# Metaformer block with a delta-rule mixer: the order of the first tiles' projections, statistics and norms around chunk 0

## The chip, the cores and the metric

One Trainium2 chip, one of its cores. Five engines run their own in-order instruction streams and meet at semaphores: TensorE (PE), VectorE (DVE), ScalarE (ACT), GpSimd (POOL) and the queue of DMA issues (SP). The metric is the device time of one execution in microseconds, and the figure given for a kernel is the median of its timed runs.

## The reference, cut to what matters

The input x is [8, 192, 16, 16]: 8 batches, 192 channels, 256 positions. All is float32.

```python
# 1. mixer: LayerNorm over channels, then a delta rule in 12 heads of width 16
q = l2norm(heads(silu(t @ Wq))); k = l2norm(heads(silu(t @ Wk)))
v = heads(silu(t @ Wv));         beta = sigmoid(t @ Wb)
# per head, for each position: u = beta*(v - S^T k);  S = S + k u^T;  o = S^T q
x = x + (t + o @ Wo)
# 2. feed-forward: LayerNorm, 8 experts with the top 2 taken, one shared expert of width 768
g = silu(x @ w_gate[e]) * (x @ w_up[e]);  routed = sum_e gate[e] * (g @ w_down[e])
out = x + alpha * shared + (1 - alpha) * routed
```

## The kernel before, in words

The 256 positions are cut into 16 **tiles** of 16 positions; a tile holds 8 batches x 16 positions, 128 tokens on the 128 partitions. All engines walk the same loop `chunks(step)` (L171), with c from -3 to 18. In step c, `at(d, fn)` works on tile c + d: the first norm and the projections run three tiles ahead of the recurrence (d = 3), the head norms two ahead (d = 2), the recurrence itself is chunk c (d = 0), and the feed-forward lags one to three chunks. The order of the work in a step is written out by hand for each engine, and since each engine is in order, an instruction that waits holds all that stands behind it.

**Front of a tile a.** ACT copies x (`A_xs`), PE transposes it (`A_x`, L363, L364; it waits until the v bank has been read, so for `A_z` and `A_silu_v` of the tile before), DVE takes statistics (`A_stats` L1125, `A_mean` L1129, `A_var` L1135), POOL makes the root (`rsqrt` L952), DVE the bias (`A_bias` L1142), ACT h and the residual (`A_plus` L594, `A_h` L585, `A_xh` L600), PE transposes h (`A_h` L355), ACT and DVE split it into a high and a low part (`A_hT` L608, `A_low` L1175), and PE projects: `A_vb` (v and beta, 5 matmuls of 204 columns) into one bank, `A_qk` (q and k, 5 matmuls of 384 columns) into another.

**Norms.** ACT: `A_silu_v` (L625, waits for DVE's `A_z` L1200, since both read the v bank), `A_silu_qk` (L617, L618), `A_sq` (L629); DVE sums the squares (`A_ss` L1206); ACT loads another table and makes the inverse norms (`A_inv`, L635 to L645); POOL scales: `A_kn` (ksc L928, kn L930), `A_vn` (L920), `A_klo` (L938, the low part of k), `A_qn` (L912). SP writes k to a scratch in HBM (L242) and reads it back in the layout of the recurrence as KR (L251), the same for q (L261, L273). The head of the queue is `load` (L286): tile 0's k and q with the feed-forward weights between and behind them; from c = 0 on each step issues tile c + 1's k, x or weights, and q.

**Recurrence.** PE spreads k over the partitions with `fill(c, f)` (L403), one for each pair of positions, f from 0 to 7, into two banks in turn; fill f waits until pair f - 2 is done. DVE then runs 16 positions of four operations: product (L1425), sum (L1427), product (L1429), state (L1433). They are numbered as slots 0 to 63, position i having slots 4i to 4i + 3, and `others(slot)` (L1310) puts DVE's work for other tiles behind given slots. In chunk 0, and in some slots later, each operation runs in two halves. Slot 8f needs fill f, so slot 40 needs fill 5. POOL multiplies states by q when half a chunk is done (`reading`, L963), and sums (`summing`, L970, L987) into oT, which DVE transposes in slot 23 of the next chunk (`Fa_otok` L1238); Wo, the second norm and the experts follow from it.

**Weights.** The experts' weights are split in high and low parts in the same opening: DVE's `split_up` (L1191 cast, L1193 subtraction), ACT's `weights_hi0` and `weights_hi1`, POOL's `weights_lo0` (L993) and `weights_1` (L998). They are placed by hand between the steps above.

The orders that the change touches are PE's for c < 0 (L472), ACT's for c = -2 (L758), POOL's for c = -1 and c = 0 (L1022, L1035), DVE's slots for c < 0 and c = 0 (L1316, L1335).

Of the kernel before, what the change touches and what calls it, by code (L numbers as in the profile page):

```python
# [34 lines left out]
def build(nc, x, Wq, Wk, Wv, Wb, Wo, router_w, w_gate, w_up, w_down, ws_gate, ws_up, ws_down, sg_w, sg_b, out):  # L35
    ctx = ExitStack()
    with ctx:
# [302 lines left out]
        def _(pe):  # L340
# [129 lines left out]
            def step(c, par):  # L470
                at = partial(stage, c, par)
                if c < 0:  # L472
                    at(3, A_x)
                    at(1, fill, 0)
                    at(1, fill, 1)
                    at(1, fill, 2)
                    at(3, A_h)
                    at(1, fill, 3)
                    at(3, A_vb)
                    at(1, fill, 4)  # L480
                    at(3, A_qk)
                elif c == 0:
                    at(3, A_x)
                    at(0, fill, 5)
                    at(0, fill, 6)
                    at(0, fill, 7)
                    at(1, fill, 0)
                    at(1, fill, 1)
                    at(3, A_h)
                    at(1, fill, 2)  # L490
                    at(3, A_vb)
                    at(3, A_qk)
                elif c < NC:
                    at(-2, Fb_up, 5)
                    at(0, fill, 3)
                    at(-2, Fb_up, 6)
                    at(-3, Fb_down, 4)
                    at(-1, Fa_o)
                    at(0, fill, 4)
                    at(3, A_x)  # L500
                    at(-2, Fb_turn, 0)
                    at(-1, Fa_y)
                    at(-2, Fb_up, 7)
                    at(-2, Fb_up, 8)
                    at(0, fill, 5)
                    at(-2, Fb_up, 9)
                    at(-2, Fb_up, 10)
                    at(-1, Fa_h)
                    at(-3, Fc_out)
                    at(-2, Fb_turn, 1)  # L510
                    at(-2, Fb_up, 11)
                    at(0, fill, 6)
                    at(-1, Fb_up, 0)
                    at(-2, Fb_turn, 2)
                    at(-2, Fb_down, 0)
                    at(0, fill, 7)
                    at(-2, Fb_down, 1)
                    at(-2, Fb_turn, 3)
                    at(-2, Fb_down, 2)
                    at(1, fill, 0)  # L520
                    at(-1, Fb_up, 1)
                    at(-1, Fb_up, 2)
                    at(3, A_h)
                    at(1, fill, 1)
                    at(-2, Fb_turn, 4)
                    at(-2, Fb_down, 3)
                    at(-1, Fb_up, 3)
                    at(1, fill, 2)
                    at(-1, Fb_up, 4)
                    at(3, A_qk)  # L530
                    at(3, A_vb)
                else:
                    at(-3, Fb_down, 4)
                    at(-2, Fb_up, 5)
                    at(-1, Fa_o)
                    at(-2, Fb_up, 6)
                    at(-2, Fb_turn, 0)
                    at(-1, Fa_y)
                    at(-2, Fb_up, 7)
                    at(-2, Fb_up, 8)  # L540
                    at(-2, Fb_turn, 1)
                    at(-3, Fc_out)
                    at(-2, Fb_up, 9)
                    at(-2, Fb_up, 10)
                    at(-1, Fa_h)
                    at(-2, Fb_down, 0)
                    at(-2, Fb_up, 11)
                    at(-1, Fb_up, 0)
                    at(-2, Fb_turn, 2)
                    at(-2, Fb_down, 1)  # L550
                    at(-1, Fb_up, 1)
                    at(-2, Fb_turn, 3)
                    at(-2, Fb_down, 2)
                    at(-1, Fb_up, 2)
                    at(-2, Fb_turn, 4)
                    at(-2, Fb_down, 3)
                    at(-1, Fb_up, 3)
                    at(-1, Fb_up, 4)
# [5 lines left out]
        def _(act):  # L564
# [179 lines left out]
            def step(c, par):  # L744
# [12 lines left out]
                    at(3, A_hT)  # L757
                elif c == -2:  # L758
                    at(3, A_xs)
                    at(2, A_silu_v)  # L760
                    at(2, A_silu_qk)
                    at(2, A_sq)
                    table(0, LN_EXP)
                    at(2, A_inv)
                    at(2, A_khi)
# [132 lines left out]
        def _(pool):  # L898
# [111 lines left out]
            def step(c, par):  # L1010
# [9 lines left out]
                    weights_lo0(5)  # L1020
                    weights_lo0(6)
                elif c == -1:  # L1022
                    rsqrt(c)
                    weights_lo0(7)
                    weights_lo0(8)
                    at(2, A_vn)
                    at(2, A_kn)
                    weights_lo0(9)
                    at(2, A_klo)
                    at(2, A_qn)  # L1030
                    weights_lo0(10)
                    weights_lo0(11)
                    weights_1(0)
                    weights_1(1)
                elif c == 0:  # L1035
                    weights_1(2)
                    weights_1(3)
                    at(0, reading, 0)
                    rsqrt(c)
                    weights_1(4)  # L1040
                    at(0, summing, 0)
                    at(2, A_vn)
                    at(2, A_kn)
                    weights_1(5)
                    at(2, A_klo)
                    at(0, reading, 1)
                    at(2, A_qn)
                    at(0, summing, 1)
                    weights_1(6)
                    weights_1(7)  # L1050
                    weights_1(8)
                elif c < NC:
                    once(c, 1, weights_1, 9)
                    at(-2, hidden, 6)
                    if c <= NC:
                        rsqrt(c)
                    at(-2, hidden, 7)
                    once(c, 1, weights_1, 10)
                    once(c, 1, weights_1, 11)
                    at(0, reading, 0)  # L1060
                    at(-2, hidden, 8)
                    at(-2, hidden, 9)
                    at(-2, hidden, 10)
                    at(0, summing, 0)
                    at(2, A_kn)
                    at(-2, hidden, 11)
                    at(2, A_qn)
                    at(-1, hidden, 0)
                    at(0, reading, 1)
                    at(0, summing, 1)  # L1070
                    at(2, A_vn)
                    at(-1, hidden, 1)
                    at(-1, hidden, 2)
                    at(-1, hidden, 3)
                    at(-1, hidden, 4)
                    at(-1, hidden, 5)
                    at(2, A_klo)
                else:
                    at(-2, hidden, 6)
                    if c <= NC:  # L1080
                        rsqrt(c)
                    at(-2, hidden, 7)
                    at(-2, hidden, 8)
                    at(-2, hidden, 9)
                    at(-2, hidden, 10)
                    at(-2, hidden, 11)
                    at(-1, hidden, 0)
                    at(-1, hidden, 1)
                    at(-1, hidden, 2)
                    at(-1, hidden, 3)  # L1090
                    at(-1, hidden, 4)
                    at(-1, hidden, 5)
# [20 lines left out]
        def _(dve):  # L1113
# [193 lines left out]
            def step(c, par):  # L1307
                w.clear()

                def others(done):  # L1310

                    def at(slot, d, fn, *args):
                        if done == slot:
                            stage(c, par, d, fn, *args)

                    if c < 0:  # L1316
# [3 lines left out]
                        at(11, 2, A_low)  # L1320
                        if c == -1 and done == 12:
                            split_up(3)
                        at(17, 2, A_z)
                        if c == -1 and done == 18:
                            split_up(4)
                        at(24, 3, A_stats)
                        at(27, 3, A_mean)
                        at(28, 3, A_var)
                        if c < -1:
                            at(35, 2, A_ss)  # L1330
                            at(48, 3, A_bias)
                        if c == -2 and done == 50:
                            split_up(0)
                            split_up(1)
                    elif c == 0:  # L1335
                        at(1, 1, A_ss)
                        at(3, 2, A_bias)
                        at(10, 1, A_vT)
                        at(20, 2, A_low)
                        at(27, 2, A_z)  # L1340
                        at(36, 3, A_stats)
                        at(38, 3, A_mean)
                        at(39, 3, A_var)
                        at(43, 2, A_ss)
                        at(50, 3, A_bias)
                    elif c < NC:
                        at(8, 2, A_low)
                        at(19, 2, A_z)
# [125 lines left out]
```

## Time and profile before

| | us |
|---|---|
| median of 3 timed runs | 482.03 (480.83 to 482.60) |
| the profiled execution | 479.88 |
| its span in the trace | 478.1 |
| first product of chunk 0 on DVE | 28.41 |
| DVE busy, of the span | 420.2 (88%) |
| POOL busy | 407.4 (85%) |
| PE busy | 414.6 (87%) |
| ACT busy | 345.8 (72%) |

The page's row of DVE by tenths in 40 slices of 12 us is `4489989999999999999999999999999999996200`. It is filled from the third slice on, and empties in the last three. The opening, from 0 to about 78 us, is where the change lies. To read it, take the timeline of one engine, name each instruction's tile by its place in the order written out above, and look at the bracket behind it: the idle time before it and what ended that.

### The profile page before, as it was taken

To read this page: it belongs to the slowest core of one execution; us is meant where nothing else is said; L and a number is where in the kernel's file an instruction comes from. 1 tells how busy PE (TensorE), PEld (TensorE's weight loads), DVE (VectorE), ACT (ScalarE), POOL (GpSimd) and SP (SyncE) were. 2 spreads that over 40 slices of the span, in tenths; PEclk is the share of its full clock that TensorE was granted. 3 is DMA by queue.
4 is the path that set the end of the run, shared out by engine and by line. 5 is a ranking of instruction groups with operands and counts; after the bars stand their busy time and mean duration, and the time that the engine had idled before them with its cause. 6 is when DMAs were issued, how large, how long until landed. Compare 5 with 4: busy or idle time off the path is not lost.

```text
span 478.1 us, 10362 instructions
## 1 busy us (share of the span) xinstructions
PE 414.6 (87%) x2400; PEld 384.1 (80%) x2400; DVE 420.2 (88%) x2268; ACT 345.8 (72%) x998; POOL 407.4 (85%) x520
## 2 busy tenths in 40 slices
PE   1354456899999999999999999999999989899996
PEld 0333336798999999899999999999999979799895
DVE  4489989999999999999999999999999999996200
ACT  3699656585969787878778786969695848475762
POOL 4379888899999999999999999999999999986340
PEclk9998555999999999999999999999999999999999
DMA  6655673732233223232332323323322232200301
GB/s 162 169 129 124 147 187 84 179 91 83 80 84 91 81 78 92 72 92 63 93 81 76 98 71 90 85 83 93 83 73 92 77 95 86 89 1 1 116 2 16
DMA packets 43437, 42.91 MB, mean 90 GB/s; under 512 B 20144, under 2 KB 35184, under 8 KB 43376
## 3 DMA queue, kind: packets, MB, share of 16 engines
q1 hardware_dynamic: 42768, 42.05, 33.2%
q8 instruction: 19, 0.31, 0.3%
q14 instruction: 42, 0.34, 0.3%
q10 hardware_dynamic: 608, 0.21, 0.2%
HBM read 35.95 MB, written 6.29 MB: 88 GB/s over the span
## 4 chain that ended last, share of the span: by engine, by line
DVE 67%; PE 13%; issue 7%; SPq 4%; DMA 4%; ACT 2%; POOL 1%; DVEq 0%; ACTq 0%; POOLq 0%
DVE Pr L1425 15%; DVE bank L1429 15%; DVE u L1427 14%; DVE SH L1433 12%; PE bank L463 3%; DMA k_scratch<-khl 2%; PE bank L436 1%; PE bank L448 1%; DVE ss L1206 1%; SPq L242 1%; DMA q_scratch<-qn 1%; PE bank L440 1%; DVE vT L1213 1%; DVE otok L1238 1%; PE bank L438 1%
## 5 line engine op out<-in xcount | busy, mean ns | idle before, releaser
L1008 POOL TENSOR_TENSOR hid<-sg,ug 128x192 f32<-128x192 f32 x192 | 112.9, 608 | 21.2 <-ACT ug L714 18.0
L963 POOL TENSOR_TENSOR PQ<-SH,QB 128x768 f32<-128x768 f32 x62 | 112.7, 1840 | 0.9 <-DVE SH L1433 0.9
L713 ACT ACTIVATE sg<-bank 128x192 f32<-128x192 f32 x192 | 64.3, 335 | 60.7 <-PE bank L440 49.1
L970 POOL TENSOR_TENSOR PQ<-PQ 128x768 f32<-128x768 f32 (+2 forms) x93 | 103.0, 1107 | 6.0
L463 PE MATMUL bank<-Wd,hidT 128*128 128x192 f32 x576 | 106.6, 326 | 0.0
L1429 DVE TENSOR_TENSOR bank<-bank,u 128x96 f32<-128x96 f32 (+1 forms) x467 | 104.1, 263 | 0.6
L1427 DVE TENSOR_REDUCE u<-Pr 128x6 f32<-128x102 f32 (+1 forms) x437 | 102.1, 267 | 0.4
L1425 DVE TENSOR_TENSOR Pr<-SH,bank 128x96 f32<-128x96 f32 (+1 forms) x437 | 100.7, 264 | 1.7 <-issue 0.3
L1433 DVE TENSOR_TENSOR SH<-SH,bank 128x96 f32<-128x96 f32 (+1 forms) x467 | 101.5, 254 | 0.5 <-DVE st L1125 0.2
L463 PEld LDWEIGHTS bank<-Wd,hidT 128*128 128x128 f32 x576 | 94.5, 190 | 0.0
L436 PE MATMUL bank<-Whi,hiT 128*128 128x384 f32 (+1 forms) x192 | 72.5, 377 | 1.3 <-DVE loT L1168 1.3
L403 PE MATMUL bank<-KR,Sel 128*128 128x384 f32 x128 | 54.1, 424 | 20.0 <-DVE SH L1433 13.2
L440 PE MATMUL bank<-W,loT 128*128 128x384 f32 (+1 forms) x192 | 66.0, 344 | 0.0
L439 PE MATMUL bank<-W,hiT 128*128 128x384 f32 (+1 forms) x192 | 65.7, 342 | 0.0
L438 PE MATMUL bank<-Whi,loT 128*128 128x384 f32 (+1 forms) x192 | 65.7, 342 | 0.0
L437 PE MATMUL bank<-Wlo,hiT 128*128 128x384 f32 (+1 forms) x192 | 65.5, 341 | 0.0
L714 ACT ACTIVATE ug<-bank,gate 128x192 f32<-128x192 f32 x128 | 53.4, 417 | 0.0
L448 PE MATMUL bank<-ident,hid 128*128 128x128 f32 x288 | 45.6, 276 | 8.9 <-ACT hidT L724 8.2
L748 ACT ACT_TABLE_LOAD x38 | 48.8, 1283 | 0.7
L724 ACT ACTIVATE hidT<-bank 128x512 f32<-128x512 f32 (+1 forms) x80 | 45.7, 572 | 2.2 <-PE bank L448 2.0
L448 PEld LDWEIGHTS bank<-ident,hid 128*128 128x128 f32 x288 | 33.9, 141 | 15.0 <-issue 11.8
L403 PEld LDWEIGHTS bank<-KR,Sel 128*128 128x128 f32 x128 | 25.9, 203 | 24.7 <-DVE SH L1433 16.4
(143 smaller groups left out, 814.5 us busy)
## 6 DMA issues: line engine op xcount, KB each, us to landing
QB<-q_scratch SPq DMA_DIRECT2D x64, 384.0 KB
k_scratch<-khl SPq DMA_DIRECT2D x64, 48.0 KB, 1.7
KR<-k_scratch SPq DMA_DIRECT2D x32, 96.0 KB, 2.4
q_scratch<-qn SPq DMA_DIRECT2D x64, 24.0 KB, 1.8
Wd<-in_L_ffn_w_down_dram SPq DMA_DIRECT2D x4, 288.0 KB, 9.4
out_dram<-xT SPq DMA_DIRECT2D x1, 896.0 KB, 4.1
Wlo_unsplit<-in_L_ffn_w_gate_dram SPq DMA_DIRECT2D x2, 384.0 KB, 4.6
Wlo_unsplit<-in_L_ffn_w_up_dram SPq DMA_DIRECT2D x2, 384.0 KB, 5.5
```

Source lines behind the costliest of these rows:

```text
L403: mm(bKB[f % 2][:, 0:2 * BR * G], Sel[:, f].rearrange("p b x e -> p (b x e)"), KR[:, p, :], start=True, stop=True).then_inc(s_fill, 1)
L436: mm(to, hiT[:, p, 0:P], Whi0[:, w], start=True, stop=False)
L440: mm(to, loT[:, p, P:2 * P], W1[:, w], start=False, stop=True).then_inc(s_up, 1)
L448: last = tr(bHt[:, (k - lo) * P:(k - lo + 1) * P], hid[:, k % (KT // 2) * P:(k % (KT // 2) + 1) * P], ident[:, :])
L463: last = mm(bDn[:, 0:C], hidT[:, turn_half(g), k - lo, :], Wd[:, k, :], start=False, stop=(k == KT - 1))
L963: tt(PQ[:, at * BR * HP:(at + n) * BR * HP].rearrange("p (i b h) d -> p i b (h d)", i=n, b=BR), SH[:, lo:lo + n].rearrange("p i b h d -> p ...
L970: chained(tt(PQ[:, :, 0:w], PQ[:, :, 0:w], PQ[:, :, w:2 * w], ALU.add))
L1008: tt(hid[:, r * H:(r + 1) * H], sg[:, m % RING], ug[:, m % RING], ALU.mult).then_inc(s_hid, 1)
L1425: v = each(slot, lambda lo, hi: count(tt(Pr[:, lo:hi, i, :, 0:D], prev[:, lo:hi], KB[:, lo:hi], ALU.mult)), Sb)
L1427: v = each(slot + 1, lambda lo, hi: count(nc.vector.tensor_reduce(u[:, i % 2, lo:hi], Pr[:, lo:hi, i], X, ALU.add, negate=True)), v)
L1429: v = each(slot + 2, lambda lo, hi: count(tt(KB[:, lo:hi], KB[:, lo:hi], u[:, i % 2, lo:hi].unsqueeze(3).to_broadcast([P, hi - lo, HP, D]) ...
L1433: ins = tt(SH[:, i, lo:hi], prev[:, lo:hi], KB[:, lo:hi], ALU.add)
```

## The change

PE projects q and k ahead of v and beta for tile 0; in step -1 the first two fills of chunk 0 go ahead of tile 2's x. ACT takes silu of q and k and the squares ahead of silu of v for tile 0. DVE sums tile 0's squares ahead of z. Tile 2's statistics leave step -1 and go behind slots 3, 7 and 8 of chunk 0, and what stood in chunk 0's slots moves back by four slots (its bias from 3 to 12). POOL's root for tile 2 goes behind two subtractions of weights, and tile 2's qn behind the sums of chunk 0's second half.

```diff
@@ PE, c < 0
-                    at(3, A_x)
+                    if c < -1:
+                        at(3, A_x)
                     at(1, fill, 0)
                     at(1, fill, 1)
+                    if c == -1:
+                        at(3, A_x)
                     at(1, fill, 2)
                     at(3, A_h)
                     at(1, fill, 3)
+                    if c == -3:
+                        at(3, A_qk)
                     at(3, A_vb)
                     at(1, fill, 4)
-                    at(3, A_qk)
+                    if c > -3:
+                        at(3, A_qk)
@@ ACT, c == -2
-                    at(2, A_silu_v)
                     at(2, A_silu_qk)
                     at(2, A_sq)
+                    at(2, A_silu_v)
@@ POOL, c == -1
-                    rsqrt(c)
                     weights_lo0(7)
                     weights_lo0(8)
+                    rsqrt(c)
@@ POOL, c == 0
                     at(0, reading, 1)
+                    at(0, summing, 1)
                     at(2, A_qn)
-                    at(0, summing, 1)
@@ DVE, c < 0
+                        if c < -1:
+                            at(16, 2, A_ss)
                         at(17, 2, A_z)
-                        at(24, 3, A_stats)
-                        at(27, 3, A_mean)
-                        at(28, 3, A_var)
                         if c < -1:
-                            at(35, 2, A_ss)
+                            at(24, 3, A_stats)
+                            at(27, 3, A_mean)
+                            at(28, 3, A_var)
                             at(48, 3, A_bias)
@@ DVE, c == 0
-                        at(1, 1, A_ss)
-                        at(3, 2, A_bias)
-                        at(10, 1, A_vT)
-                        at(20, 2, A_low)
-                        at(27, 2, A_z)
-                        at(36, 3, A_stats)
-                        at(38, 3, A_mean)
-                        at(39, 3, A_var)
-                        at(43, 2, A_ss)
-                        at(50, 3, A_bias)
+                        at(3, 2, A_stats)
+                        at(5, 1, A_ss)
+                        at(7, 2, A_mean)
+                        at(8, 2, A_var)
+                        at(12, 2, A_bias)
+                        at(14, 1, A_vT)
+                        at(24, 2, A_low)
+                        at(31, 2, A_z)
+                        at(40, 3, A_stats)
+                        at(42, 3, A_mean)
+                        at(43, 3, A_var)
+                        at(47, 2, A_ss)
+                        at(54, 3, A_bias)
```

## Rows read from the trace of the kernel before

**Rows 1.** Windows (stretch, length, busy time of PE, PEld, DVE, ACT, POOL, clock, DMA): steady state
```profile
100.00:300.00 200.00, 194.62 (x1187) 184.98 (x1187) 198.41 (x1102) 156.35 (x474) 190.71 (x238) 1.00 0.31 84
```
**Rows 2.** Timeline (start, duration, engine line operation, [idle before]): tile 0's projections and squares
```profile
12.25 0.51 PE L372 MATMUL bank<-Wphi,hhi 128*128 128x204 f32 x1 [1.02 <-DVE hlo L1175]
...
13.41 0.57 PE L372 MATMUL bank<-Wphi,hhi 128*128 128x384 f32 x1
...
15.88 0.52 ACT L629 ACTIVATE sq<-qk 128x384 f32<-128x384 f32 x1
...
16.50 0.54 DVE L1206 TENSOR_REDUCE ss<-sq 128x24 f32<-128x384 f32 x1
```
**Rows 3.** Timeline: tile 2's x and statistics, and chunk 0's first fill and product
```profile
26.94 0.45 PE L363 MATMUL bank<-ident,xs 128*128 128x128 f32 x1 [0.48 <-ACT v L625]
...
27.61 1.01 PE L403 MATMUL bank<-KR,Sel 128*128 128x384 f32 x2
...
28.34 0.15 DVE L1135 TENSOR_SCALAR ve<-mv 128x1 f32<-128x1 f32 x1
28.41 0.42 DVE L1425 TENSOR_TENSOR Pr<-SH,bank 128x96 f32<-128x96 f32 x2
```
**Rows 4.** Timeline: POOL's and DVE's operations on SBUF, side by side and alone
```profile
18.78 0.56 DVE L1193 TENSOR_TENSOR Wlo<-Wlo_unsplit,Whi 128x384 fp32r<-128x384 f32 x1
18.81 0.61 POOL L928 TENSOR_TENSOR ksc<-inv 128x12 f32<-128x12 f32 x1 [1.46 <-ACT inv L645]
...
23.61 1.24 DVE L1193 TENSOR_TENSOR Wlo<-Wlo_unsplit,Whi 128x384 fp32r<-128x384 f32 x1
...
31.60 0.21 POOL L928 TENSOR_TENSOR ksc<-inv 128x12 f32<-128x12 f32 x1
```
**Rows 5.** Timeline: SP's transfers of k, and chunk 2's first fill and product
```profile
24.18 1.20 SPq L251 DMA_DIRECT2D KR<-k_scratch  x2
...
35.85 4.86 SPq L242 DMA_DIRECT2D k_scratch<-khl  x4
...
74.04 1.19 SPq L251 DMA_DIRECT2D KR<-k_scratch  x2
...
77.22 0.69 PE L403 MATMUL bank<-KR,Sel 128*128 128x384 f32 x1 [3.82 <-DMA KR<-k_scratch]
...
78.02 0.41 DVE L1425 TENSOR_TENSOR Pr<-SH,bank 128x96 f32<-128x96 f32 x2
```
**Rows 6.** Timeline: ACT, PE, and DVE's slots 32, 36 and 40 in chunk 0
```profile
30.39 0.28 ACT L594 ACTIVATE rstd<-rs,one 128x1 f32<-128x1 f32 x1
...
32.44 0.36 ACT L742 ACTIVATE khl<-kn 128x192 fp32r<-128x192 f32 x1 [0.26 <-POOL kn L930]
...
39.78 0.33 ACT L625 ACTIVATE v<-bank 128x192 f32<-128x192 f32 x1
...
40.48 0.42 DVE L1425 TENSOR_TENSOR Pr<-SH,bank 128x96 f32<-128x96 f32 x2
...
40.75 0.45 PE L403 MATMUL bank<-KR,Sel 128*128 128x384 f32 x1
...
41.81 0.41 DVE L1425 TENSOR_TENSOR Pr<-SH,bank 128x96 f32<-128x96 f32 x2
...
43.52 0.41 DVE L1425 TENSOR_TENSOR Pr<-SH,bank 128x96 f32<-128x96 f32 x2
```
**Rows 7.** Timeline: POOL in chunk 0 and at the start of chunk 1
```profile
31.13 0.51 POOL L920 TENSOR_TENSOR vn<-v,inv 128x192 f32<-128x192 f32 x1
...
40.59 3.59 POOL L963 TENSOR_TENSOR PQ<-SH,QB 128x768 f32<-128x768 f32 x2 [0.55 <-DVE SH L1433]
...
52.22 3.58 POOL L963 TENSOR_TENSOR PQ<-SH,QB 128x768 f32<-128x768 f32 x2
...
56.90 0.51 POOL L912 TENSOR_TENSOR qn<-qk,inv 128x192 f32<-128x192 f32 x1 [1.10 <-DMA q_scratch<-qn]
...
61.29 0.38 DVE L1238 STREAM_TRANSPOSE otok<-oT 128x192 f32<-128x192 f32 x1 [0.65 <-POOL oT L987]
```

## The prediction

> **What bounds the kernel now.** I read the windows first, then the timeline of the opening engine by engine, then the rows at the borders of chunks 0, 1 and 2. In the steady state DVE is busy for 198.41 of 200 us [rows 1], so once chunk 2 runs, nothing but DVE counts, and the change touches no work there. Whatever the change does must be seen as a shift of chunk 2's first product, now at 78.02 [rows 5]. Three chains meet in the opening:
> - **DVE**: chunk 0 starts at 28.41 [rows 3] and then has no gap until it waits 0.65 us for oT, POOL's sums of chunk 0, at 61.29 [rows 7].
> - **POOL**: it waits once, 0.55 us, for half of chunk 0 at 40.59, and then works without a gap to the products at 52.22, which end at 55.80. qn of tile 2 then waits 1.10 us for a write of the scratch and starts at 56.90; the sums stand behind it, so the wait at 61.29 is theirs [rows 7].
> - **SP**: the two reads of KR go out from 24.18, and from there SP issues without a gap to tile 1's k at 35.85; that write, the x, and tile 2's k follow one another by DMA landings until chunk 2's KR is issued at 74.04. Fill 0 of chunk 2 starts at 77.22, the moment it lands, and ends at 77.91, 0.11 us ahead of the product that needs it [rows 5].
>
> The last one decides what can be won. DVE may come as early as it likes to chunk 2; without KR it can start there at about 77.95. **So the change can win 0.1 us at most, plus what it takes off tile 0's k**, as nothing in it alters what SP issues or how much the DMAs move.
>
> **Tile 0's k.** q and k are projected first. Their group starts at 12.25 in place of 13.41, 1.16 us earlier [rows 2], so the squares end at 16.40 - 1.16 = 15.24. But silu of v now stands between the squares and the table load, and it waits for z, which waits on DVE for the sum of squares. So: sum from 15.3, 0.54 [rows 2]; z with the step to ACT some 0.25 (an estimate, from 0.15 for ve [rows 3]); silu 0.33 [rows 6]. The table load would start at about 16.4, which is where it can start now, behind the squares [rows 2]. The 1.16 us are gone: worth 0.0, between -0.3 and +0.2.
>
> PE's x of tile 1 waits for that silu, so it starts at 16.55, 0.15 behind it, the step that tile 2's x shows. From x at 26.94 to the end of the variance at 28.49 are 1.55 us [rows 3], so the root of 0.7 us would run from 18.2 to 18.9. It stands ahead of ksc on POOL, which starts at 18.81 now [rows 4]: +0.1.
>
> The larger term is what the root releases. DVE's bias waits for it and holds the two weight splits (four operations on SBUF, 1.8 us in all), which today end at 19.34, just when k's scaling starts; they would now run from 19.1 to 21, beside ksc, kn, vn and klo. The trace shows what that costs: ksc took 0.61 beside the last of them (18.78 to 19.34) and 0.21 without; a split of 0.56 took 1.24 beside POOL [rows 4]. Each of kn, vn and klo may wait for the rest of a DVE operation of 0.35 to 0.56, half of one on average: 3 x 0.25 = 0.75, less the 0.40 that ksc no longer loses, plus the 0.1 of the root, is +0.45. Bounds are -0.3 (no collision, ksc at 0.21) and +1.0 (each waits a whole one). I take **+0.5**.
>
> The Trainium skill (SBUF — State Buffer, Who interferes with whom) says that a DVE operation with two SBUF inputs, or a cast in a two-port mode, and a GpSimd operation that reads SBUF hold one shared port pair in turn, each for its whole instruction. By that rule the two streams alternate, and +0.5 to +0.9 would be the outcome; the rows at 18.81 and 23.61 agree [rows 4].
>
> **The first fills.** KR's second half lands 3.18 us behind its first issue (74.04 to 77.22 [rows 5]), so chunk 0's is there at about 27.3, while its fill starts at 27.61, behind tile 2's x. The fill alone takes 0.69 [rows 5], the product could start at 28.0: 0.4 earlier than 28.41 [rows 3]. With the +0.5 of tile 0's k it starts at **28.5**, 0.1 later than now. DVE must be free by then; today it waits for tile 2's x, from 26.94 on [rows 3], and the late splits take most of that. I put this at 0, with up to +0.4.
>
> **Tile 2's statistics in chunk 0.** Operations behind slots are not free, as chunk 0 has no gap. The same three operations for tile 3 lie between slots 36 and 40, which take 1.71 us (41.81 to 43.52), while slots 32 to 36 take 1.33 (40.48 to 41.81) [rows 6]: **+0.4**. The other moved ones keep their price, four slots later (1.33 us).
>
> **What waits for them.** The variance of tile 2 now ends 3.95 us into chunk 0 (nine slots of 0.33, the statistics' 0.4, tile 1's sum of squares 0.45, its own 0.15), at 32.4; the root follows at 32.5 in place of about 28.6 [rows 3], and ACT's rstd at 33.3, 2.9 us later than 30.39 [rows 6]. ACT had no slack but 0.26 us ahead of khl [rows 6], so all its work behind shifts by 2.6 us: tile 2's silu of v ends at 42.7 in place of 40.11. PE's x of tile 3 waits for it (as it does now, at 40.11), and **fill 5 stands behind that x**. From the end of that silu to the end of fill 5 it takes 1.1 us now (40.11 to 41.20 [rows 6]); tile 2's x and the fill behind it took 1.4 from x to end (26.94 to 27.61 + 0.69 [rows 3, 5]), 1.5 with the step: fill 5 is ready at 43.8 to 44.2. Slot 40 needs it. It starts at 43.52 now, of which 0.40 is tile 3's statistics, which move behind it; with the 0.1 and tile 2's 0.4 that is 43.6 [rows 6]. The stall is 0.2 to 0.6; I take **+0.45**. Chunk 0 then ends 0.1 + 0.4 + 0.45 = 0.95 later, at about 53.1.
>
> POOL: vn of tile 1 stands behind the root, so it starts at 33.2 in place of 31.13. From there to the products at 40.59 POOL has 8.9 us of work and 0.55 of idle time, so these start at 42.1, and it is POOL, no longer DVE, that sets them. To the second products are 11.63 us [rows 7], and 0.5 more where klo of tile 2 waits for ACT's late khl: 42.1 + 12.1 = 54.3, and they end at 57.8. **qn behind the sums** now saves its wait and its 0.51: the sums start at once (57.9 in place of 57.4) and take 3.85 to the end of oT (57.4 to 61.25, just ahead of otok [rows 7]): 61.8. otok is at **61.9** in place of 61.29. So the 1.6 us that the swap takes out of POOL's chain are spent by the late root. DVE, coming to that slot at 61.6, waits 0.3.
>
> **Sum.** +0.1 (start) + 0.4 (statistics) + 0.45 (fill 5) = +0.95 on DVE, of which the smaller wait for oT gives back 0.35: +0.6 at otok. All behind it, the wait for the second norm included, keeps its distance to otok. Chunk 2 starts at 78.6; KR allows 78.45. Rounded up for DVE's crowded front: **+0.7 us**. The profiled execution would take 479.88 + 0.7 = 480.6. The timed runs' median, 482.03, lies 2.15 above it, so the median after is **482.7**. About 0.5% (2.4 us) is what a measurement of this kernel can tell from no change.
>
> **Rivals.**
> 1. *The starts are won.* POOL takes its three operations between DVE's, ksc costs 0.21, and ACT catches up before fill 5. Chunk 0 starts at 27.7 to 28.0, oT is there at 60 and DVE no longer waits for it. Then KR bounds chunk 2, at 77.6 to 77.95: -0.1 to -0.4, a median of 481.6 to 481.9. For it speaks that each cause of delay has under 1 us; against it that all of them sit on ACT and POOL, which have no gaps there. Chance 0.25.
> 2. *Slower: fill 5 behind tile 3's x.* It decides from the point where tile 2's silu of v ends later than about 42.4; every further microsecond of ACT is one of DVE and then of POOL. If the splits push tile 0's k by 1.0 and chunk 0's start by 0.4 beyond that, khl of tile 1 also misses SP's slot at 35.85 and moves all later k. That gives +1.5 to +3, a median of 483.5 to 485. Chance 0.15.
> 3. *The DMA landings shift.* From tile 1's k at 35.85 to chunk 2's KR at 74.04 [rows 5] SP's way lies over landings beside weights and x; were they to land 2.5 us or more earlier, KR would no longer cap. Nothing alters its neighbours in the queue. Chance 0.03, -2.5 or so.
>
> The forecast keeps 0.57. The range goes from 480.6 (rival 1 less the spread of 1 us of the runs) to 485.0. Faster by over 0.5%: 0.04 (rival 3 and stray). Slower: 0.08, the upper half of rival 2. The same: 0.88.
>
> **What would show it.** Tile 0's table load at 16.3 to 16.5; k's first write at 21.5 to 21.8 in place of 21.16, with stretched kn, vn, klo; chunk 0's first product at 28.4 to 28.6; a wait of DVE ahead of slot 40; POOL's products at 42; no wait of qn; otok near 61.9; chunk 2's KR fill at 77.7. A chunk 2 that starts ahead of 77.5, or a chunk 0 that starts ahead of 27.6, would show the argument wrong.

## The result and the profile after

The changed kernel takes **482.45 us** (median of 22 runs, 482.05 to 482.97); the kernel before, run beside it, 481.21 us (22 runs, 479.59 to 482.60). The ratio is **1.0035, with a 95% interval of 1.0025 to 1.0044**: slower, by about 1.2 to 1.7 us, and within the 0.5% of the forecast's middle case. The two ranges say more than the medians. The shortest run of the kernel before is 2.5 us below the shortest of the changed one, and its runs spread over 3.0 us, those of the changed kernel over 0.9. The profiled executions took 479.88 and 482.4 us, spans 478.1 and 480.7.

In the steady state nothing has changed. The window from 100 to 300 us of the changed kernel (columns as in [rows 1]):

```profile
100.00:300.00 200.00, 194.72 (x1187) 184.58 (x1186) 198.38 (x1103) 155.88 (x473) 190.50 (x239) 1.00 0.30 84
```

DVE is busy for 198.38 of 200 us against 198.41 [rows 1]. So the difference is made in the opening. The product at 78.02, which the rows and the prediction call chunk 2's first [rows 5], is chunk 1's last: it is the sixteenth from 52.12 on, where chunk 1 starts (slot 60). It starts at 80.18 in the changed kernel, 2.16 us later. Chunk 2 starts one position behind it. Timeline of the kernel before: chunk 2's first product, its fill 1, and the product of its position 2, which needs that fill:

```profile
79.38 0.42 DVE L1425 TENSOR_TENSOR Pr<-SH,bank 128x96 f32<-128x96 f32 x2
...
81.19 0.51 PE L403 MATMUL bank<-KR,Sel 128*128 128x384 f32 x1
...
82.05 0.42 DVE L1425 TENSOR_TENSOR Pr<-SH,bank 128x96 f32<-128x96 f32 x2
```

Of the changed kernel, chunk 1's last product and chunk 2's first:

```profile
80.18 0.41 DVE L1435 TENSOR_TENSOR Pr<-SH,bank 128x96 f32<-128x96 f32 x2
...
81.56 0.42 DVE L1435 TENSOR_TENSOR Pr<-SH,bank 128x96 f32<-128x96 f32 x2
```

Chunk 2 starts 2.18 us later, of a span that is 2.6 longer. The other 0.4 lies behind it (0.28 between the first products of chunks 3 and 15, 302.65 us against 302.37) and is not explained.

Timeline of the changed kernel (start, duration, engine line operation, [idle before]), tile 0's norms and the scaling of its k, to be held against [rows 2] and [rows 4]:

```profile
15.41 0.55 DVE L1212 TENSOR_REDUCE ss<-sq 128x24 f32<-128x384 f32 x1 [3.26 <-ACT sq L635]
15.88 0.16 DVE L1206 TENSOR_SCALAR zc<-bank 128x12 f32<-128x12 f32 x1
16.13 0.33 ACT L631 ACTIVATE v<-bank 128x192 f32<-128x192 f32 x1 [0.76 <-DVE zc L1206]
16.48 1.28 ACT L754 ACT_TABLE_LOAD   x1
...
18.89 0.21 POOL L934 TENSOR_TENSOR ksc<-inv 128x12 f32<-128x12 f32 x1
...
19.18 0.63 POOL L936 TENSOR_TENSOR kn<-qk,ksc 128x192 f32<-128x192 f32 x1
19.48 0.76 DVE L1199 TENSOR_TENSOR Wlo<-Wlo_unsplit,Whi 128x394 fp32r<-128x394 f32 x1
19.78 0.83 POOL L926 TENSOR_TENSOR vn<-v,inv 128x192 f32<-128x192 f32 x1
...
20.57 0.70 POOL L944 TENSOR_TENSOR khl<-kn,khl 128x192 fp32r<-128x192 f32 x1
...
21.30 1.77 SPq L242 DMA_DIRECT2D k_scratch<-khl  x4
```

The squares end early, and then the sum, z and silu of v stand one behind the other ahead of the table load: it starts at 16.48, against 16.42 in the kernel before. The k write goes out 0.14 us later than at 21.16.

The same timeline from chunk 0's start to chunk 2's, against [rows 3], [rows 5], [rows 6] and [rows 7]:

```profile
28.29 0.42 DVE L1435 TENSOR_TENSOR Pr<-SH,bank 128x96 f32<-128x96 f32 x2 [1.00 <-PE bank L403]
...
32.28 0.69 POOL L958 TENSOR_TENSOR rs<-ve,neg_half 128x2 f32<-128x2 f32 x1 [4.13 <-DVE ve L1141]
...
33.01 0.29 ACT L600 ACTIVATE rstd<-rs,one 128x1 f32<-128x1 f32 x1 [1.06 <-POOL rs L958]
...
41.94 3.61 POOL L969 TENSOR_TENSOR PQ<-SH,QB 128x768 f32<-128x768 f32 x2
...
43.99 0.42 DVE L1435 TENSOR_TENSOR Pr<-SH,bank 128x96 f32<-128x96 f32 x2 [0.72 <-PE bank L403]
...
54.15 3.59 POOL L969 TENSOR_TENSOR PQ<-SH,QB 128x768 f32<-128x768 f32 x2
...
57.81 3.46 POOL L976 TENSOR_TENSOR PQ<-PQ 128x768 f32<-128x768 f32 x3
...
61.66 0.51 POOL L918 TENSOR_TENSOR qn<-qk,inv 128x192 f32<-128x192 f32 x1
61.74 0.38 DVE L1244 STREAM_TRANSPOSE otok<-oT 128x192 f32<-128x192 f32 x1 [0.24 <-POOL oT L993]
...
62.34 0.33 ACT L623 ACTIVATE qk<-bank 128x192 f32<-128x192 f32 x1 [4.34 <-POOL qn L918]
...
63.04 0.30 PE L350 MATMUL bank<-ident,otok 128*128 128x128 f32 x1 [3.18 <-ACT qk L624]
...
64.77 0.28 ACT L665 ACTIVATE oc<-bank 128x128 f32<-128x128 f32 x1
...
67.94 0.37 DVE L1152 BATCH_NORM_STATS2 st<-bank 128x6 f32<-128x192 f32 x1 [2.24 <-PE bank L418]
...
72.45 1.20 SPq L251 DMA_DIRECT2D KR<-k_scratch  x2
```

Chunk 0 starts 0.12 us earlier (28.41 [rows 3]), the root of tile 2 holds POOL for 4.13 us and ACT for 1.06, DVE waits 0.72 us ahead of slot 40, and otok stands at 61.74 in place of 61.29 [rows 7]: 0.45 us lost so far. Then comes the larger part. **ACT waits 4.34 us for qn**, PE's transposes of o wait for the silu of q and k behind it, and the second norm's statistics start 6.20 us behind otok.

The copy of o and the second norm's statistics in the kernel before, where silu of q and k does not wait for POOL (timeline):

```profile
62.45 0.28 ACT L659 ACTIVATE oc<-bank 128x128 f32<-128x128 f32 x1 [1.33 <-PE bank L351]
...
65.79 0.37 DVE L1146 BATCH_NORM_STATS2 st<-bank 128x6 f32<-128x192 f32 x1 [0.83 <-PE bank L418]
```

There the statistics are 4.50 us behind otok: 1.70 us of the 2.16.

### The profile page after: what moved, and what is told of

It is laid out like the page before. It is cut to its first block, busy times and chain, and to the rows that moved or that the text cites. A ratio compares the mean times of both kernels' runs of the same rounds, so it can differ in the third digit from the quotient of the medians.

```text
span 480.7 us, 10362 instructions
## 1 busy us (share of the span) xinstructions
PE 415.5 (86%) x2400; PEld 384.3 (80%) x2400; DVE 421.3 (88%) x2268; ACT 345.5 (72%) x998; POOL 408.2 (85%) x520
## 4 chain that ended last, share of the span: by engine, by line
DVE 70%; PE 13%; issue 7%; ACT 4%; POOL 3%; DMA 2%; SPq 0%; DVEq 0%; ACTq 0%; POOLq 0%
DVE Pr L1435 16%; DVE bank L1439 16%; DVE u L1437 14%; DVE SH L1443 12%; PE bank L463 3%; DVE ss L1212 1%; PE bank L436 1%; PE bank L448 1%; DVE vT L1219 1%; DVE otok L1244 1%; PE bank L440 1%; PE bank L438 1%; PE bank L437 1%; PE bank L439 1%; ACT L754 1%
## 5 line engine op out<-in xcount | busy, mean ns | idle before, releaser
L1014 POOL TENSOR_TENSOR hid<-sg,ug 128x192 f32<-128x192 f32 x192 | 112.9, 608 | 21.7 <-ACT ug L720 18.3
L403 PE MATMUL bank<-KR,Sel 128*128 128x384 f32 x128 | 54.3, 427 | 16.5 <-DVE SH L1443 15.4
L439 PE MATMUL bank<-W,hiT 128*128 128x384 f32 (+1 forms) x192 | 65.7, 342 | 0.0
L438 PE MATMUL bank<-Whi,loT 128*128 128x384 f32 (+1 forms) x192 | 65.7, 342 | 0.0
```

The costliest lines, as they stand in the source:

```text
L403: mm(bKB[f % 2][:, 0:2 * BR * G], Sel[:, f].rearrange("p b x e -> p (b x e)"), KR[:, p, :], start=True, stop=True).then_inc(s_fill, 1)
L1014: tt(hid[:, r * H:(r + 1) * H], sg[:, m % RING], ug[:, m % RING], ALU.mult).then_inc(s_hid, 1)
```

## The experiments

Two distances are read in each trace, both from the start of the first matmul of tile 0's projections, called the origin below (12.25 before, 12.29 after, 12.16 to 12.71 in the experiments). The **chain** ends with the second norm's statistics of chunk 0, the row at 65.79 or 67.94; chunk 1's last product follows 12.23 us later (78.02 - 65.79 before, 80.18 - 67.94 = 12.24 after), chunk 2's first 13.6 us, and the product of its position 2 16.26 us (82.05 - 65.79). **KR** is the arrival of chunk 2's KR: the start of the fill 0 that waited for it, or an estimate where none did, its first issue + 3.18; "under" marks the two whose second read took longer to issue (the pair 1.87 and 1.99 us instead of 1.2), and gives the start of a fill 0 that waited for DVE and not for KR.

A late KR holds DVE through fill 1 first. PE is in order, and between the two fills of chunk 2 stand the next ten matmuls of the up-projection and two transposes: fill 1 starts 3.97 us behind a fill 0 that waited (77.22 and 81.19 before, 78.23 and 82.20 in e1), takes up to 0.67, and 0.04 later position 2 can start. So KR counts where it is more than 11.6 us behind the chain's end (16.26 less 3.97, 0.67 and 0.04). The traces bear this out: against its 16.26 us, position 2 is late by 0.07 us in e3, 0.18 in e1, 0.30 in e5, 0.49 in e2, 1.12 in e6 (where fill 1 follows already after 3.45 us) and 1.60 in e8, and by nothing in the kernel before, where the distance is 11.43. Timeline of e2, fills 0 and 1 of chunk 2 and the product of position 2:

```profile
78.40 0.69 PE L403 MATMUL bank<-KR,Sel 128*128 128x384 f32 x1 [4.46 <-DMA KR<-k_scratch]
...
82.37 0.67 PE L403 MATMUL bank<-KR,Sel 128*128 128x384 f32 x1
...
83.08 0.42 DVE L1425 TENSOR_TENSOR Pr<-SH,bank 128x96 f32<-128x96 f32 x2 [0.40 <-PE bank L403]
```

| kernel | median us | ratio to before (95%) | chain | KR |
|---|---|---|---|---|
| before | 481.2 to 481.3 | | 53.54 | 64.97 |
| changed | 482.45 | 1.0035 (1.0025 to 1.0044) | 55.65 | 63.34 |
| e1_qn_first | 481.92 | 1.0020 (1.0002 to 1.0038) | 53.88 | 65.64 |
| e2_qn_alone | 481.59 | 1.0017 (0.9995 to 1.0038) | 53.71 | 65.78 |
| e3_fill5_first | 482.79 | 1.0040 (1.0025 to 1.0056) | 55.46 | 67.12 |
| e4_z_first | 482.07 | 1.0020 (1.0004 to 1.0036) | 54.87 | under 65.7 |
| e5_tile0_alone | 481.69 | 1.0014 (0.9993 to 1.0035) | 53.82 | 65.71 |
| e6_stats_early | 482.16 | 1.0028 (1.0011 to 1.0045) | 54.57 | 68.03 |
| e7_three | 480.54 | 0.9989 (0.9972 to 1.0006) | 53.64 | under 64.5 |
| e8_four | 481.34 | 1.0013 (0.9996 to 1.0030) | 54.57 | 67.76 |
| e9_before_wd | 479.99 | 0.9982 (0.9964 to 1.0001) | | |
| e10_after_wd | 482.37 | 1.0019 (1.0005 to 1.0034) | 55.50 | 61.94 |
| e11_four_wd | 479.71 | 0.9972 (0.9955 to 0.9989) | 52.71 | 58.77 |
| e12_four_wd_q | 480.05 | 0.9982 (0.9963 to 1.0000) | 53.55 | 57.63 |

The experiments have 12 runs each. The intervals are 0.3% wide because the kernel before spreads, so differences between variants are read from the chain, and from medians of one group of runs (e1 to e4, e5 to e8, e9 to e12). The changed kernel's median is from the group of the result; the kernel before is in every group, at 481.2 to 481.3. The profiled execution of e9 was an outlier of over 2,200 us, as one other run in e2, so e9 has no chain here.

**e1_qn_first: is it the qn?**

```diff
 # changed kernel, POOL, c == 0
                     at(0, reading, 1)
+                    at(2, A_qn)
                     at(0, summing, 1)
-                    at(2, A_qn)
```

> The changed kernel with one thing undone: tile 2's qn stands ahead of the sums of chunk 0's second half again. Theory (the qn behind the sums holds ACT's silu of q and k of tile 3, which reuses qn's input buffer, and behind it the copy of chunk 0's output on ACT and the bank on PE): silu of q and k starts at about 59 instead of 62.34, the copy of o no longer waits for it, the way from otok to the second norm's statistics shrinks from 6.2 to about 4.5 us, oT comes 0.5 later, and chunk 2 starts 1.2 us earlier than in the changed kernel: 0.9 us slower than the kernel before, ratio about 1.001. Rival (the late root of tile 2 and fill 5 make the loss, the swap of qn is innocent or a gain): no faster than the changed kernel, ratio 1.0035 or more.

Timeline of e1:

```profile
58.00 0.51 POOL L918 TENSOR_TENSOR qn<-qk,inv 128x192 f32<-128x192 f32 x1
...
59.76 0.33 ACT L623 ACTIVATE qk<-bank 128x192 f32<-128x192 f32 x1 [1.57 <-PE bank L376]
...
62.39 0.38 DVE L1244 STREAM_TRANSPOSE otok<-oT 128x192 f32<-128x192 f32 x1 [0.70 <-POOL oT L993]
...
66.47 0.37 DVE L1152 BATCH_NORM_STATS2 st<-bank 128x6 f32<-128x192 f32 x1 [0.40 <-PE bank L418]
...
78.23 0.69 PE L403 MATMUL bank<-KR,Sel 128*128 128x384 f32 x1 [4.16 <-DMA KR<-k_scratch]
```

otok is 0.35 us later than in the changed kernel from the same origin (49.80 against 49.45), and the statistics 1.77 earlier: the way between them is 4.08 us instead of 6.20. ACT no longer waits for qn. The held buffer is shown by the chain, and it was worth more there than the 1.2 us expected; the ratio alone (up to 1.0038) doesn't exclude the rival's 1.0035. The median falls by less, 482.45 to 481.92. In this execution fill 0 waits for KR and 0.18 us of the gain is lost at position 2. Other runs may lose more, as they spread from 480.62 to 483.56, but no trace shows them; e9 and e10 test this.

**e2_qn_alone: what is the swap worth by itself?**

```diff
 # kernel before, POOL, c == 0
                     at(0, reading, 1)
-                    at(2, A_qn)
                     at(0, summing, 1)
+                    at(2, A_qn)
```

> The kernel before with the qn of tile 2 behind the sums and nothing else. Theory of the held buffer: oT comes 1.5 us earlier and DVE no longer waits for it, but silu of q and k of tile 3 starts at 60.3 in place of 58.7 and the copy of chunk 0's output on ACT only about 0.3 us later than before, so the second norm's statistics stay where they are or come 0.3 later: ratio 1.000 to 1.001. Rival (the wait for oT is what counts): 0.65 us faster, ratio 0.9986.

The chain is 53.71 against 53.54: +0.17, within the 0.0 to 0.3 expected. oT comes 1.5 us earlier (59.75 with the origin at 12.62), DVE no longer waits for it, and gets nothing. Silu of q and k of tile 3 starts at 60.73 behind qn, the copy of o at 63.16. So the swap is worth nothing in the kernel before and costs 1.8 us in the changed one, where qn comes 1.9 us later from the origin (49.37 against 47.43). The rival (0.65 us faster) falls by the chain; the ratio alone, 0.9995 to 1.0038, also excludes 0.9986.

**e3_fill5_first: does DVE's stall in chunk 0 count?**

```diff
 # changed kernel, PE, c == 0
-                    at(3, A_x)
                     at(0, fill, 5)
+                    at(3, A_x)
```

> The changed kernel with PE's fill 5 of chunk 0 ahead of tile 3's x. It removes the 0.72 us that DVE waits ahead of slot 40. Theory (after the late root POOL and ACT set when oT comes, DVE has slack): chunk 1 starts 0.7 us earlier, oT and chunk 2's start stay within 0.1 us, ratio as the changed kernel, 1.0035. Rival (each stall of DVE in chunk 0 counts in full): 0.7 us faster than the changed kernel, ratio 1.002.

The wait ahead of slot 40 is gone, and DVE waits for oT instead. Timeline of e3:

```profile
61.97 0.38 DVE L1244 STREAM_TRANSPOSE otok<-oT 128x192 f32<-128x192 f32 x1 [0.92 <-POOL oT L993]
```

0.92 in place of 0.24: 0.68 of the 0.72 us come back as another wait. The chain is 0.19 shorter, the ratio 1.0040. In this kernel the stall cost little, as POOL was later still.

**e4_z_first: what eats the early projection?**

```diff
 # changed kernel, DVE, c < -1
+                            at(15, 2, A_z)
                             at(16, 2, A_ss)
-                        at(17, 2, A_z)
```

(for c == -1, z stays behind slot 17)

> The changed kernel with DVE's z of tile 0 ahead of the sum of squares. Theory (in the changed kernel silu of v stands between the squares and the table load and waits for the sum and z behind it, which eats what the projection of q and k first wins): silu of v runs from 15.45, the table load starts at 15.8 in place of 16.48, tile 0's k is written 0.6 us earlier, chunk 0 starts at 27.65 in place of 28.29, and chunk 2 starts 0.6 us earlier than in the changed kernel: ratio 1.002. Rival (collisions of DVE and POOL at SBUF or the DMA landings set chunk 0's start): under 0.2 us, ratio 1.0035.

Timeline of e4, its first projection at 12.28:

```profile
15.28 0.17 DVE L1206 TENSOR_SCALAR zc<-bank 128x12 f32<-128x12 f32 x1 [3.15 <-PE bank L376]
15.39 0.55 DVE L1212 TENSOR_REDUCE ss<-sq 128x24 f32<-128x384 f32 x1
15.54 0.33 ACT L631 ACTIVATE v<-bank 128x192 f32<-128x192 f32 x1 [0.19 <-DVE zc L1206]
15.89 1.28 ACT L754 ACT_TABLE_LOAD   x1
...
20.71 1.77 SPq L242 DMA_DIRECT2D k_scratch<-khl  x4
```

z now ends before the sum starts; table load and k write are 0.59 us earlier, the chain 0.78 us shorter, the ratio 1.0020. The theory's numbers hold: z behind the sum made the first part of the change worthless.

**e5_tile0_alone: the first part of the change on the kernel before.**

```diff
 # kernel before: PE c == -3, ACT c == -2, DVE c < -1, as in the change
-  A_vb(0), A_qk(0)              +  A_qk(0), A_vb(0)
-  silu_v, silu_qk, sq           +  silu_qk, sq, silu_v
-  z, stats(1), ..., ss          +  ss, z, stats(1), ...
```

> The kernel before with the first part of the change alone: q and k of tile 0 projected first, ACT's silu of q and k and squares ahead of silu of v, DVE's sum ahead of z, in step -2. Theory (z and silu of v stand in the way of the table load): the load starts at the same distance from the first projection as before (4.2 us), k of tile 0 is written 0.1 to 0.3 us later as the weight splits run beside its scaling, and the time is that of the kernel before or 0.3 us longer: ratio 1.000 to 1.001. Rival (the 1.16 us by which q and k come earlier reach the k write): 0.5 us or more faster, ratio 0.999.

The table load stands at 16.79 with the origin at 12.61: 4.18 us, before 4.17. The k write is at 9.01 us from the origin, before 8.91; the chain is 53.82, +0.28. Nothing won, as the theory has it.

**e6_stats_early: what is the late root of tile 2 worth?**

```diff
 # changed kernel, DVE, c == 0
-                        at(3, 2, A_stats)
-                        at(5, 1, A_ss)
-                        at(7, 2, A_mean)
-                        at(8, 2, A_var)
-                        at(12, 2, A_bias)
+                        at(2, 2, A_stats)
+                        at(3, 2, A_mean)
+                        at(4, 2, A_var)
+                        at(5, 1, A_ss)
+                        at(8, 2, A_bias)
 # vT(1) at 11, low(2) 21, z(2) 28, stats(3) 38, mean 40, var 41, ss(2) 45, bias(3) 52
```

> The changed kernel with other slots in chunk 0: tile 2's statistics behind slots 2, 3 and 4 in place of 3, 7 and 8, its bias behind 8 in place of 12, and the rest one to three slots earlier. Theory (the late root of tile 2 holds ACT and POOL, and these set oT and with it everything up to chunk 2): the root starts 1.4 us earlier, ACT and POOL behind it run 0.7 to 0.8 us earlier (they also need the sum of tile 1's squares), fill 5 is ready in time, POOL's first products start 0.75 us earlier, and the time falls by 0.7 us against the changed kernel: ratio 1.002. Rival (POOL's and ACT's queues are late for other reasons): as the changed kernel, 1.0035.

Timeline of e6, its first projection at 12.40:

```profile
66.97 0.37 DVE L1152 BATCH_NORM_STATS2 st<-bank 128x6 f32<-128x192 f32 x1 [2.24 <-PE bank L418]
...
77.33 1.19 SPq L251 DMA_DIRECT2D KR<-k_scratch  x2
...
80.43 0.69 PE L403 MATMUL bank<-KR,Sel 128*128 128x384 f32 x1 [5.85 <-DMA KR<-k_scratch]
...
81.15 0.42 DVE L1435 TENSOR_TENSOR Pr<-SH,bank 128x96 f32<-128x96 f32 x2 [0.54 <-PE bank L403]
```

The chain is 1.08 us shorter, somewhat more than the 0.7 expected. The median falls by 0.3 only, and this execution is longer than the changed kernel's (482.76 against 482.4): KR arrives at 80.43, and chunk 2's first product, at 81.15, waits for its fill. The late statistics and root of tile 2 are worth 1.1 us of the chain together with the stall ahead of slot 40, which is gone here too and was worth 0.19 in e3. The ratio alone (1.0011 to 1.0045) doesn't exclude the rival.

**e7_three and e8_four: do the parts add up?** e7 is the changed kernel with the edits of e1, e3 and e4; e8 has those of e6 too.

> The changed kernel with qn of tile 2 ahead of the sums again, fill 5 ahead of tile 3's x, and z of tile 0 ahead of the sum of squares. Theory: the three are separate waits (1.6 us, 0.0 and 0.8 us of the 2.1 us by which chunk 2 starts later), so they add up: chunk 2 starts 0.2 to 0.3 us earlier than in the kernel before, ratio 0.9995. Rival (with the qn undone the arrival of chunk 2's KR is the bound, whatever DVE does): as with the qn undone alone, ratio 1.001 to 1.002.

> As the kernel with the three edits, and with tile 2's statistics behind slots 2, 3 and 4 too. Theory: 0.7 us less again, at most until chunk 2's KR arrives, which is itself 0.6 us earlier by the k write of tile 0: 0.6 to 1.0 us faster than the kernel before, ratio 0.998. Rival (KR's arrival bounds, at the distance from the k write that the kernel before shows): ratio 0.9995 or more.

e7: the chain is 53.64, +0.10 to the kernel before; the three edits took 2.01 us out of 2.11, less than the sum of e1, e3 and e4 (1.77 + 0.19 + 0.78). Its ratio excludes the rival's 1.001 to 1.002; the median, 480.54, is below that of the kernel before, but the interval holds 1. Its runs lie within 1.3 us (480.07 to 481.33). e8 missed its theory (0.998), and its 1.0013 is what the rival said, 0.9995 or more: its runs spread from 479.99 to 483.78. In its profile qn waits 1.87 us for the landing of tile 1's q write, and chunk 2's fill 0 for KR until 80.07, which costs position 2 1.60 us. KR comes 59.3 us behind tile 0's k write there and 56.1 in the kernel before, so it does not keep a distance to that write, as the rival had it.

**e9 to e12: the second chain.** Chunk 2's KR depends on writes and reads that share the DMAs with the weights. Its arrival, from the same program on SP, lies anywhere from 63.3 to 68.0 in the table's upper rows. The last four kernels move three loads of weights out of its way:

```diff
 # SP, steps 0 and 1
                     at(1, scratch_q)
+                    for i in range(3):
+                        once(c, 1, load_down, i)
                     at(1, spread_q)
-                for i in range(KT // 3):
-                    once(c, i // 3, load_down, i)
+                for i in range(3, KT // 3):
+                    once(c, 1, load_down, i)
```

e9 is the kernel before with it, e10 the changed kernel, e11 is e8 with it, and e12 is e11 with `scratch_q` ahead of `load_later` in step 0.

> The kernel before with the first three loads of the down-projection weights taken from in front of tile 2's k write and put behind chunk 2's KR and q write. Theory (the kernel before has two chains that end at chunk 2's start: DVE's, which would give the 479.2 to 479.8 us of its shortest runs, and the arrival of chunk 2's KR, which differs by several us from run to run and sets the longer ones): KR arrives 3 us or more ahead of its fill, the median falls to 479.4 to 480.0, the runs lie within 1.5 us instead of 3 to 4.7, ratio 0.997. Rival (the spread of the kernel before has its cause elsewhere): the same median and spread, ratio 1.000.

> The changed kernel with the same three loads moved. Theory: in the changed kernel the chain over qn, ACT and the second norm ends behind KR's arrival in nearly all runs, so nothing is won: 482.0 to 482.5, ratio 1.0025 to the kernel before, and against the kernel before with the same move the whole price of the change shows: 2.1 to 2.8 us. Rival (the transfers cost the changed kernel as much as the kernel before): 1.5 us faster, ratio 0.9995.

> The kernel with the four edits (z first, fill 5 first, qn ahead of the sums, statistics early) with the same three loads moved. Theory: without the late KR (80.07 in its profile) chunk 2 starts at its own chain's time, which is still tied to the landing of tile 1's q write, for which qn waits: 479.0 to 480.2, ratio 0.996 to 0.997. Rival (the four edits have nothing left to give): as the kernel before with the move, or slower.

> The same, with tile 1's q write issued ahead of the rest of x. Theory: the write lands near 50 instead of 56 to 58, qn of tile 2 no longer waits for it (1.87 us in the profile with the four edits), oT comes 1.3 to 1.9 us earlier and the time falls by 0.8 to 1.5 us against the last kernel: ratio 0.994 to 0.995. Rival (x arrives 2 us later, tile 4's x on ACT and behind it silu of q and k of tile 3 and the copy of chunk 0's output take its place as the bound): as the last kernel or slower.

e9 falls to 479.99, and all its runs but the outlier lie in 479.34 to 481.32, where the kernel before beside it has 478.91 to 483.23 and one outlier. That is a spread of 2.0 us, more than the 1.5 expected, and the interval of its ratio just holds 1. e10 stays at 482.37 (482.17 to 482.85), and its shortest run is longer than the longest of e9. So KR hardly ever counted in the changed kernel. In the kernel before, 16 of 34 runs are longer than e9's longest, and KR's arrival is the likely cause; as e9 has no trace of a usual run, its earlier KR is inferred from e10 (61.94) and e11 (58.77). With the loads moved **the change costs 2.4 us** (482.37 - 479.99), which is what the two profiled executions show (2.5), and twice the difference of the medians.

Timeline of e11, its first projection at 12.58:

```profile
56.39 0.51 POOL L920 TENSOR_TENSOR qn<-qk,inv 128x192 f32<-128x192 f32 x1
...
60.78 0.38 DVE L1246 STREAM_TRANSPOSE otok<-oT 128x192 f32<-128x192 f32 x1
...
65.29 0.37 DVE L1154 BATCH_NORM_STATS2 st<-bank 128x6 f32<-128x192 f32 x1 [0.83 <-PE bank L420]
...
68.17 1.19 SPq L251 DMA_DIRECT2D KR<-k_scratch  x2
```

qn does not wait here, KR is issued at 68.17 instead of 72 to 77, and the chain is the shortest of all, 52.71. **e11 is faster than both kernels, by 0.1 to 0.5% than the one before: 0.9972 (0.9955 to 0.9989)**. It differs from e8 by the moved loads alone, and its KR comes 9.0 us earlier (58.77 against 67.76). Against e9 it gains 0.3 us of the median, which these runs can't separate from nothing; so most of its gain is the moved loads. e12 shows its rival: x lands later, ACT waits 3.31 us for it in the profile, and the copy of o comes 1.0 us later from the origin (50.39 against 49.36). Moving the q write ahead of x is no gain.

## Why the prediction was right, and where a step failed

The range (480.6 to 485.0) holds 482.45, the sign (+0.7) is right, and "the same within 0.5%" came out. The parts up to otok were right in kind and nearly in size. The larger part of the loss, 1.70 of 2.16 us, was not foreseen, and that the median came out so close is luck. By steps:

- **The first part is worth nothing**: right. The table load was put at 16.4 and stands at 16.48; e4 and e5 show the reason.
- **k write +0.5**: too much; +0.14, or +0.10 from the origin. ksc moved from 18.81 to 18.89, which is the later table load more than the root: it starts 0.10 behind the end of the inverse norms, against 0.08. ksc did lose its 0.40. kn, vn and khl stretched from 0.51, 0.51 and 0.59 to 0.63, 0.83 and 0.70, 0.55 together. From the start of kn to the k write it is 0.46 more than before (2.12 against 1.66), where the sum had 0.75; 0.08 - 0.40 + 0.46 is the 0.14. The Trainium skill's rule of one port pair in turn (SBUF — State Buffer, Who interferes with whom) agrees in that both sides stretch, DVE's split to 0.76 as well; that the two would wait out whole instructions, +0.5 to +0.9, the trace does not bear out.
- **Start of chunk 0 at 28.5**: 28.29. **Statistics in slots, +0.4, and fill 5, +0.45**: chunk 0 took 24.68 us (28.29 to 52.97) against 23.71 (28.41 to 52.12), so 0.25 for the first, as the stall of 0.72 is the rest. Their sum was 0.85, and is 0.97.
- **POOL after the late root**: products at 42.1 and 54.3, measured 41.94 and 54.15; oT at 61.8, measured 61.70; otok at 61.9, measured 61.74. The wait that decides is the root's, as forecast: e6 takes 1.08 us out of the chain with it, and e3 shows that DVE's own stall is at most 0.19 of that.
- **"All behind it, the wait for the second norm included, keeps its distance to otok": wrong, and the step that failed.** It became 6.20 us instead of 4.50. I had asked who waits for oT, not who waits for qn. `A_silu_qk` of the next tile waits for qn (its `s_qn` wait, since both use the buffer qk), `Fa_o` on PE waits for that silu (its `s_qks` wait; the row at 63.04), and ACT's copy of o stands behind silu, squares, silu of v and a weight split. e1, which moves qn alone, gives 1.77 us of the chain back.
- **KR caps the gain at 0.1 us**: that KR is a second bound is right. The working is wrong in two ways. The product at 78.02 doesn't need fill 0 of chunk 2: it is chunk 1's last, and chunk 2's first, at 79.38, has 1.47 us to spare behind the fill's end at 77.91. What KR bounds is position 2, through fill 1, and that leaves 0.15 us in this execution (11.58 - 11.43), so the size of the cap was right by luck. And I took one arrival (77.22) for a schedule. It moves by up to 4.7 us between the profiled executions of kernels with the same program on SP (table). The median of 482.03 that I started from, 2.15 us above the profile, was a sign of it, and I treated the gap as a constant to be added. For the changed kernel there is no such gap (482.4 profiled, 482.45 median), so the two errors, 1.8 us too little (+0.7 for +2.5) and 2.1 us too much, nearly cancelled in the absolute time: luck, not skill. The shift against the kernel before, +0.7, was too small whichever way it is counted: +1.2 by the medians, +2.4 with KR out of the way.
- Of the rivals, the second (slower through fill 5 behind x) has its stall, 0.72 us, but its +1.5 to +3 was to come from there; the 2.4 us had another path.

What stays open: why the arrival of KR differs so much between executions of one program. Only that the weights in front of the k write have a part in it is shown (67.76 in e8, 58.77 in e11).

## What to carry to other kernels

When an instruction moves behind a long one on its engine, list all who wait for its completion, the waits that only free its input buffer too: here ACT and PE waited for an operation whose result nobody needed yet. When the profile and the median differ by more than the spread of a quiet variant (2.15 us against 0.9 here), look for a second chain that ends close to the first and varies; a change to the first is then priced by a variant in which the varying one is taken out of the way. A stall that is removed only counts if what DVE waits for next is there earlier too: 0.68 of 0.72 us came back in e3. And count the positions before you name a product: the bound of KR was read one product too early.

## What the runs showed of the hardware

- The way of k through HBM is the variable part of this opening: tile 1's KR read is issued at 45.05 to 48.75 us in these profiles, tile 2's at 66.6 to 77.3, though the first k write goes out at 20.6 to 21.7 in all of them.
- The clock of TensorE fell to 1.2 GHz (granted 0.50) from 44 us on in the kernel before, and stayed at 2.4 GHz (granted 1.00) until beyond 60 in the changed one. A single fill behind an idle stretch took 0.69 us at either level (the ones at 50.29 before and 47.16 after), and matmuls of 384 columns follow each other every 0.32 us at either (from 58.05 to 59.01 in the changed kernel at 1.00, from 78.34 to 80.91 in the kernel before at 0.50). Windows of the changed and of the kernel before:

```profile
44.00:52.00 8.00, 1.61 (x3) 0.57 (x2) 8.00 (x48) 7.64 (x17) 7.31 (x9) 1.00 0.53 136
```

```profile
44.00:52.00 8.00, 1.48 (x3) 0.58 (x2) 8.00 (x48) 7.10 (x16) 7.61 (x12) 0.50 0.43 115
```

The busy times of PE are nearly the same in the two. Ahead of this stretch, from 42 to 44 us, PE was busy for 1.41 us in the changed kernel and for 0.41 in the kernel before. The clock doesn't explain the loss: the kernel that had the lower one from 44 to 60 us is the faster.
